# Attention block with feed-forward part on eight cores: the value matmuls of a key tile issued one key tile earlier

## The reference

```python
h = (x - mu) * rsqrt(var + 1e-05) * ln_gamma + ln_beta
q, k, v = split_heads(h @ w_qkv + b_qkv)          # 16 heads of 64
attn = softmax(q @ k.T / sqrt(64))                # over 4096 keys
a = x + ((attn @ v) @ w_out + b_out)
x = layernorm(x + a)
s = x @ Win + bin_                                # 64 columns
g = einsum(relu(s[..., None] * W1 + b1), W2) + b2
x = layernorm(x + g @ Wout + bout)
```

## Time and profile before

| what | value |
|---|---|
| time, median of 3 runs | 2216.4 us |
| lowest and highest of them | 2131.49 and 2253.01 us |
| the profiled execution | 2128.16 us |
| its span on the slowest core (core 2) | 2126.6 us |
| spans of the eight cores | 2111.5 to 2126.6 us |
| mean granted TensorE clock, by core | 0.874 to 0.885 |
| attention stage, first to last exponential | 275.7 to 1785.5 us |

### The profile page before, as it was taken

The page is one execution under the profiler, slowest core; times in us unless marked ns, Lnnn a source line. Parts: engine busy times, 40 slices in busy tenths (PEclk is TensorE's granted clock), DMA queues, the critical chain, the costliest instruction groups (busy, mean ns, idle before and its releaser), DMA issues. The chain is left out here.

```text
span 2126.6 us, 26829 instructions; the slowest of 8 cores (2111.5 to 2126.6 us)
## 1 busy us (share of the span) xinstructions
PE 1438.1 (68%) x8552; PEld 509.5 (24%) x8552; DVE 607.9 (29%) x806; ACT 1360.3 (64%) x1478; POOL 26.1 (1%) x35
## 2 busy tenths in 40 slices
PE   0443378868977986888689678858875764464343
PEld 0221123313322332232233223312321221122111
DVE  2333212231222133122212322231222010345554
ACT  3777377858876875788588767858876885022222
POOL 0000000000000000000000000000000000000000
PEclk9766589989999999999899989999998998666555
DMA  6222000000010001001000100010000002402202
GB/s 107 79 80 80 0 1 6 5 6 6 1 11 1 6 1 11 1 6 11 1 6 1 11 1 6 1 10 1 6 1 1 1 1 55 74 0 79 56 24 80
DMA packets 44598, 44.36 MB, mean 21 GB/s; under 512 B 34993, under 2 KB 35122, under 8 KB 44466
## 3 DMA queue, kind: packets, MB, share of 16 engines
q1 hardware_dynamic: 16162, 33.72, 5.4%
q0 software_dynamic: 28304, 8.92, 4.2%
HBM read 43.16 MB, written 8.39 MB: 24 GB/s over the span
## 5 line engine op out<-in xcount | busy, mean ns | idle before, releaser
L833 ACT ACTIVATE PT_sb<-score_ps,negB_sb 128x1024 bf16<-128x1024 f32 x1024 | 1140.9, 1114 | 292.8 <-PE z_ps L775 154.5
L749 PE MATMUL score_ps<-qT_sb,kT_sb 64*128 64x512 bf16 x1024 | 397.5, 392 | 243.5 <-ACT PT_sb L833 150.9
L765 PE MATMUL pv_ps<-PT_sb,v_sb 128*64 128x512 bf16 x1024 | 405.4, 396 | 41.9 <-DVE attnT_sb L791 27.3
L769 PE MATMUL pv_ps<-PT_sb,v_sb 128*64 128x512 bf16 x1024 | 406.5, 397 | 0.0
L751 PE MATMUL score_ps<-qT_sb,kT_sb 64*128 64x512 bf16 x1024 | 401.7, 396 | 0.0
L775 PE MATMUL z_ps<-PT_sb,onesb_sb 128*64 128x512 bf16 x1024 | 393.8, 385 | 0.0
L772 PE MATMUL z_ps<-PT_sb,onesb_sb 128*64 128x512 bf16 x1024 | 393.7, 384 | 0.0
L604 PE MATMUL qkv_ps<-xhq_sb,wq_sb 128*128 128x512 bf16 x1120 | 300.4, 392 | 10.5 <-DVE qT_sb L619 5.3
L749 PEld LDWEIGHTS score_ps<-qT_sb,kT_sb 64*128 64x128 bf16 x1024 | 94.0, 93 | 626.1 <-issue 625.3
L765 PEld LDWEIGHTS pv_ps<-PT_sb,v_sb 128*64 128x64 bf16 x1024 | 111.6, 109 | 218.6 <-issue 167.9
L788 DVE RECIPROCAL zb_sb<-z_ps 128x512 f32<-128x512 f32 x32 | 107.4, 3358 | 155.7 <-PE z_ps L775 115.7
(11 more groups left out here) (80 smaller groups left out, 829.2 us busy)
## 6 DMA issues: line engine op xcount, KB each, us to landing
xtile_sb<-x SPq DMA_DIRECT2D x32, 512.0 KB, 3.7
xres_sb<-x SPq DMA_DIRECT2D x16, 512.0 KB, 8.2
out<-u_sb SPq DMA_DIRECT2D x16, 512.0 KB, 4.3
wq_sb<-wqkv POOLq DMA_DIRECT2D x24, 256.0 KB, 5.6
wout_sb<-wout POOLq DMA_DIRECT2D x1, 2048.0 KB, 23.0
win_sb<-win POOLq DMA_DIRECT2D x1, 128.0 KB, 23.2
rw_sb<-rw POOLq DMA_DIRECT2D x1, 128.0 KB, 23.1
w2b_sb<-w2b POOLq DMA_DIRECT2D x1, 128.0 KB, 23.1
```

Source lines behind the costliest of these rows:

```text
L749: e.matmul(o, w, r, start=True, stop=True))
L765: a=s0, b=s1: e.matmul(o, w, r, start=a, stop=b, skip_group_check=True))
L769: e.matmul(o, w, r, start=a, stop=b, skip_group_check=True))
L833: e.activation(out=o, in_=i_, func=AF.Exp, bias=b, scale=0.125))
```

## The change

The value groups are issued one key tile earlier. At an odd `kt` the kernel before issues those of `kt - 3` and `kt - 2`; the changed one those of `kt - 2` and `kt - 1`. At `kt` 1, where none was issued, value group 0 now is, alone. `finish_qt` has one group left, that of key tile 31, in place of two.

```diff
     def finish_qt(h, pqt, hit):
         sc.wait("tensor", ss, h["exp_done"][NKT - 1])
-        for j in (NKT - 2, NKT - 1):
-            h["pvz_done"][j] = emit_pvz(pqt, j, hit, h["exp_done"])
+        h["pvz_done"][NKT - 1] = emit_pvz(pqt, NKT - 1, hit, h["exp_done"])
...
-            if kt % 2 == 1 and kt >= 3:
-                pvz_done[kt - 3] = emit_pvz(qt, kt - 3, it, exp_done)
-                pvz_done[kt - 2] = emit_pvz(qt, kt - 2, it, exp_done)
+            if kt % 2 == 1:
+                if kt >= 2:
+                    pvz_done[kt - 2] = emit_pvz(qt, kt - 2, it, exp_done)
+                pvz_done[kt - 1] = emit_pvz(qt, kt - 1, it, exp_done)
```

## The result

The changed kernel took 2168.2 us (median of 10 runs), the kernel before 2129.07 us (median of 10): 1.0193 of it, with a 95% interval from 1.0168 to 1.0218. By that ratio it is 41 us slower, by the two medians 39. The ratio leaves out executions in which one half of the chip was granted a lower clock, and two of the three executions behind the prediction's median of 2216.4 were such ones; over ten the median lies beside the profiled execution, so the sum is compared here with its own figure, +14.8 us. The profiled execution's span went from 2126.6 to 2164.6 us.

A forecast was written before the change was run, and what follows sets the result against it. ACT should bound the steady part but also waited for value groups; -26.9 + 29.8 - 3.9 + 15.8 = +14.8 us on 2128.16 gave 2143.0 us (scaled to the median, 2232), range 2120 to 2285.

The forecast's parts named there:

- the clock dips at every boundary: Sign of being wrong: the granted clock dips at every query-tile boundary, where the forecast had about half of them.
- Term A: Steady part with projections: exponentials stop waiting for value groups, 0.32 us saved in six, 84 times, -26.9 us.
- Term B: Query-tile boundaries: value group 0 waits with later matmuls behind it, 1.24 us later at each of 24, +29.8 us.
- the walk: Step-by-step timing of PE and ACT over one query-tile boundary, before and after; exponential 6 comes 1.24 us later.
- Term C: End of each of eight subgroups: one value group fewer behind the last exponential, 8 x 0.49 = -3.9 us.
- Term D: Slow clock after PE's 2.98 us gap at half of 21 boundaries, 1.5 us a fall, +15.8 us.
- the clock falls in every one of the 21 gaps and stays low for two stretches: Rival at boundaries with projections: slow clock costs 2.9 us each, +60 us in sum, 2188 us; chance 0.20.
- the three cases in the earlier trace: Clock around PE's near-idle times: 1.00 from 946, 0.50 from 847, 0.77 then 0.52 after 1668.
- The sentence on the Trainium skill: Idle gaps bring the slow clock back; by that rule alone every boundary falls, 21 x 1.5 = 31.5 us.
- The naive rival: Value-group waits really hold ACT, in row-maximum steps too, and boundaries cost nothing: -62 us, 2066 us; chance 0.05.

The follow-up runs named there:

- e3_filler: The changed kernel with 34 dummy transposes on PE ahead of value group 0 of each query tile but a subgroup's first; 2118.02 us, 0.9958 of the kernel before.
- e9_mix: e1_v0_back with value group 0 at kt 1 in each subgroup's first query tile, as in the changed kernel; 2080.21 us, repeated 2081.23 us, 0.9788 of the kernel before.
- e1_v0_back: The changed kernel with value group 0 put back at kt 3, all else as changed; 2090.24 us, 0.9825 of the kernel before.

## Why the prediction was right and wrong

The forecast was +0.7%, within 2%; measured were +1.9%, the right direction with nearly three times the size. Of the signs of being wrong that the prediction names, one came: the clock dips at every boundary.

**Term A, the steady part (-26.9 us).** Right. A block of 27 exponentials at 1.21; from E(10) to E(28) 22.67 became 21.72, which is 0.95, three times 0.32. The reason held as well: the exponential's wait for V(k-4) is gone and ACT is the next bound. The row-maximum stretch kept its pace of 3.4 us a pair, as forecast.

**Term B, the order at the boundary (+29.8 us).** Right, as e3_filler shows: with the clock kept up, E(3) to E(6) come as in the walk (1.29 us in place of 1.24 at the 21 boundaries with projections, 0.4 to 0.6 at the three of the last subgroup), and the second and third tiles come out even.

**Term C, the subgroup's end (-3.9 us).** Right in size: from S(31) to the first row-maximum matmul behind the last value group it was 839.24 to 843.29, 4.05 us, and is 1050.54 to 1054.16, 3.62. Left out was the subgroup's start, which makes up most of the 8 us by which e3_filler (-9 us) beats the sum of A, B and C (-1.0 us). ACT there, before and after; the first row is E(0) to E(3), the second E(4):

```profile
852.99 4.73 ACT L833 ACTIVATE PT_sb<-score_ps,negB_sb 128x1024 bf16<-128x1024 f32 x4 [0.59 <-DVE negB_sb L720]
...
859.58 1.11 ACT L833 ACTIVATE PT_sb<-score_ps,negB_sb 128x1024 bf16<-128x1024 f32 x1 [1.85 <-PE z_ps L775]
```

```profile
1063.86 4.73 ACT L833 ACTIVATE PT_sb<-score_ps,negB_sb 128x1024 bf16<-128x1024 f32 x4 [0.59 <-DVE negB_sb L720]
...
1069.59 1.11 ACT L833 ACTIVATE PT_sb<-score_ps,negB_sb 128x1024 bf16<-128x1024 f32 x1 [0.99 <-PE score_ps L751]
```

E(4) came 2.97 us after E(3), behind two value groups at the slow clock; now it is 1.8 to 2.1 us. The clock has the larger part in this too. A subgroup starts at the low level, and over its six middle starts and all eight cores that lasted until 7.0 us after E(0) before, and until 5.0 after. Where it lasted equally long, 7 to 8 us, E(0) to E(6) took 9.1 us in the kernel before and 9.3 in e9_mix, which has value group 0 in the same place as the changed one there: no gain. In all runs of kernels with value group 0 at `kt` 1 of the first tile the low level ended at 5.0 to 5.8 us in the mean, in all others at 6.9 to 7.9. e1_v0_back and e9_mix differ in this place alone. So the early value group brings the full clock back sooner, and the gain comes with that; what in it does so was not tested.

**Term D, the clock (+15.8 us).** This step failed, in its count and in its length. I let the clock fall at half of the 21 boundaries; it fell at every one, and at the last subgroup's three. And I took each low level for 3.4 us long, at 1.5 us a fall. That price was right for such a fall (1.4 to 1.6 measured), but at twelve of the 21 boundaries the low level lasted twice as long and cost 2.6 to 2.8. The measured term is 50 us. The rival "the clock falls in every one of the 21 gaps and stays low for two stretches", with +60 us, named the mechanism and nearly the size, and I gave it 0.20.

What led me to halve it was a wrong reading of the three cases in the earlier trace rows. I placed the new gap of 2.98 us between a case that fell and one that didn't. But PE's longest single gap was 1.49 us ahead of the fall at 847 and 1.09 us ahead of the one at 1669, and the gap around 946, where nothing fell, was 1.52: the new gap is longer than all three, and the cases are not in the order of their gaps. They differ in what PE did around them. It was busy for 1.19 us of the four from 1665, in which the last subgroup has no bursts, and for 2.48 of the four from 944. In the changed kernel it is 1.34 of the four from 1106, ahead of the fall shown above. The low level at 847, taken for "nearly twice as long" as 3.4 us, lasted from 846.9 to 860.6, 13.7 us.

The sentence on the Trainium skill ("TensorE: Matmul & The Clock Gate", Part 1: the slow clock is the default, activity releases it) had pointed that way; with a fall at every boundary it gave 31.5 us, still short, since the low level's length was the other error. The trace after agrees with it: a fall at all 24.

The naive rival, that the waits on value groups are what holds ACT, is refuted in the plainest way: they went from 154.5 us to 1.1 and ACT's idle time rose.

## What to carry to other kernels

A wait that is moved ahead on an in-order engine takes along all that now stands behind it: look for what ran in its shade, here two score pairs and four matmuls in that of a 3.36 us reciprocal. Give an accumulator's first write, which waits for the readers of the last round, its own place in the loop, apart from the steady rhythm. And on TensorE price a gap twice, once as time and once as clock: here the late start cost about 30 us by the sum and the slow clock 50 by e3_filler, and cheap dummy work in the gap bought the second back.

## What was not expected of the hardware

How much the clock's answer to a gap hangs on where the gap lies. Falls of the granted clock, with PE's longest empty time at the boundary, on all eight cores; the columns are the boundaries ahead of the second and fourth query tile of a subgroup with projections, ahead of its third one, and the three of the last subgroup:

| kernel | second and fourth tile | third tile | last subgroup |
|---|---|---|---|
| before | 0.8 to 1.05 us: 5 of 112 | 1.3 to 1.5 us: 0 of 56 | 0.9 to 1.1 us: 22 of 24 |
| e1_v0_back | 0.8 to 1.05 us: 0 of 112 | 1.3 to 1.5 us: 0 of 56 | 0.8 us: 24 of 24 |
| 34 transposes | 0.9 us: 0 of 112 | 1.4 us: 0 of 56 | 1.2 us: 0 of 24 |
| twelve transposes | 2.1 us: 17 of 112 | 2.6 us: 3 of 56 | 2.4 us: 23 of 24 |
| wait behind score pair 3 | 2.7 us: 108 of 112 | 2.5 to 2.8 us: 39 of 56 | 2.1 us: 24 of 24 |
| value group 0 alone | 2.9 us: 112 of 112 | 3.4 us: 50 of 56 | 3.6 us: 24 of 24 |
| changed | 2.9 us: 112 of 112 | 3.4 us: 56 of 56 | 3.2 us: 24 of 24 |

Down a column a longer gap means more falls, save in the last one, where gaps of 0.8 us fall every time and those of 1.2 us behind 34 transposes never. Across a row it does not: the third tile's gap is mostly the longest among the boundaries with projections, and where the clock does not fall at all of them it falls there least. So the length of one gap alone does not foretell a fall; what else PE does around it counts too. After each of the 192 falls in the changed kernel the low level lasted 3.4 or 6.8 us (6.7 by the rounded clock of the windows). Twelve transposes of a 128 x 128 tile, 0.84 us, kept the clock up at 19 of the 24 boundaries of the slowest core.
